# Value and query products of a tile taken in turns into two PSUM banks, in a two-layer attention kernel

## What is computed

```python
xn = layernorm(x) * norm_scale + norm_bias
q, k, v = xn @ Wq + bq, xn @ Wk + bk, xn @ Wv + bv
k, v = masked(k, -inf or -1e6), masked(v, 0)
q = softmax(q per head, over its features)
k = softmax(k per head, over the tokens)
attn = einsum('bhse,bhsd->bhed', k, v)
y = einsum('bhtd,bhed->bhte', q, attn)
scale, shift = split(silu(cond) @ film_emb_W + film_emb_b, 2)
h = layernorm(y) * film_norm_scale + film_norm_bias, then h * (1 + scale) + shift
x = x + silu(h) @ film_out_W + film_out_b
```

## Time and profile before

| | |
|---|---|
| time, median of 3 runs (lowest, highest) | 977.77 us (977.76, 980.23) |
| profiled execution, span from its first to its last instruction | 978.8 us; no time of its own is given beside the span |
| PE busy, weight loads busy | 949.3 us (97%), 819.8 us (84%) |
| DVE, ACT, POOL busy | 828.2 us (85%), 400.9 us (41%), 338.6 us (35%) |
| granted clock, mean over the span | 0.994 |
| chain that ended last, by engine | PE 90%, DVE 4%, issue 2%, others 1% or less |

### The profile page before, as it was taken

How to read it: one execution, slowest core, us unless ns; L and a number is a source line. 1 busy time by engine, 2 the same in 40 slices (tenths; PEclk the granted TensorE clock), 3 DMA queues, 4 the chain that set the end, 5 groups by cost and what they waited for, 6 DMA issues and landing times.

```text
span 978.8 us, 19392 instructions
## 1 busy us (share of the span) xinstructions
PE 949.3 (97%) x7053; PEld 819.8 (84%) x7053; DVE 828.2 (85%) x1690; ACT 400.9 (41%) x809; POOL 338.6 (35%) x441
## 2 busy tenths in 40 slices
PE   4999999999999999999989999999999999999996
PEld 3778888888888888888878888888888888888885
DVE  6799888888988888888998888888888888888865
ACT  4244343343343344334544343343344344344333
POOL 3443233333333333233534433333333333233310
PEclk9899999999999999999999999999999999999999
DMA  8760102010100000000320000000000000000001
GB/s 301 271 221 7 44 7 49 7 50 6 45 7 7 7 7 6 2 6 7 99 75 1 19 26 28 28 17 28 23 17 28 28 18 28 22 18 28 22 13 43
DMA packets 25268, 40.75 MB, mean 42 GB/s; under 512 B 1727, under 2 KB 10039, under 8 KB 25175
## 3 DMA queue, kind: packets, MB, share of 16 engines
q1 hardware_dynamic: 24672, 39.07, 12.0%
q10 hardware_dynamic: 502, 0.46, 0.2%
HBM read 31.13 MB, written 8.39 MB: 40 GB/s over the span
## 4 chain that ended last, share of the span: by engine, by line
PE 90%; DVE 4%; issue 2%; ACT 1%; DMA 1%; POOL 1%; SPq 0%; DVEq 0%; ACTq 0%; POOLq 0%
PE PS L534 69%; PE PS L614 6%; PE PS L636 3%; PE PS L603 3%; PE PS L590 3%; PE PS L575 3%; PE PS L582 3%; DMA STAGE<-in_wk 1%; PE PS L650 1%; DVE XN L754 0%; DVE WL_q L227 0%; PE PS L659 0%; DVE YN L860 0%; ACT WH_k L416 0%; DVE YN L848 0%
## 5 line engine op out<-in xcount | busy, mean ns | idle before, releaser
L421 ACT ACTIVATE EK<-PS 128x512 f32<-128x512 f32 x64 | 38.3, 598 | 391.7 <-PE PS L575 391.7
L534 PE MATMUL PS<-XH,WH_k 128*128 128x256 f32 x512 | 146.8, 287 | 4.2 <-DVE XL L764 4.2
L534 PE MATMUL PS<-XL,WH_k 128*128 128x256 f32 x512 | 146.6, 286 | 0.0
L534 PE MATMUL PS<-XH,WL_k 128*128 128x256 f32 x512 | 146.6, 286 | 0.0
L336 POOL TENSOR_SCALAR VEY<-MVY 128x1 f32<-128x1 f32 x64 | 14.6, 229 | 291.6 <-DVE MVY L855 291.5
L336 POOL TENSOR_SCALAR VEX<-MVX 128x1 f32<-128x1 f32 x64 | 17.5, 273 | 271.4 <-DVE MVX L744 271.2
L534 PE MATMUL PS<-WH_q,XH 128*128 128x512 f32 x256 | 106.4, 416 | 3.6 <-DVE WL_q L227 3.6
L534 PE MATMUL PS<-WH_o,HH 128*128 128x512 f32 x256 | 106.4, 416 | 2.4 <-ACT HH L460 2.4
L534 PEld LDWEIGHTS PS<-XH,WH_k 128*128 128x128 f32 x512 | 99.9, 195 | 7.2 <-ACT XH L479 4.6
L534 PE MATMUL PS<-WH_v,XH 128*128 128x512 f32 x256 | 105.3, 411 | 0.0
L534 PEld LDWEIGHTS PS<-XL,WH_k 128*128 128x128 f32 x512 | 99.8, 195 | 2.3
(11 more groups left out here) (117 smaller groups left out, 2224.7 us busy)
## 6 DMA issues: line engine op xcount, KB each, us to landing
out_x<-X SPq DMA_DIRECT2D x32, 256.0 KB, 2.0
X<-in_film SPq DMA_DIRECT2D x2, 2048.0 KB, 16.9
X<-in_x SPq DMA_DIRECT2D x2, 2048.0 KB, 12.0
STAGE<-in_film SPq DMA_DIRECT2D x4, 1024.0 KB, 6.4
MB<-in_mask SPq DMA_DIRECT2D x30, 128.0 KB, 2.9
X<-in_x SPq DMA_DIRECT2D x3, 1024.0 KB, 15.2
BB<-in_bias_rows SPq DMA_DIRECT2D x6, 256.0 KB, 8.2
STAGE<-in_wk SPq DMA_DIRECT2D x1, 1024.0 KB, 10.3
```

The source lines that it names most:

```text
L421: eng.activation(EK[:, :], PS[:, B_XK, :], ACT.Exp).then_inc(act_ek, 1)
L534: mm = eng.matmul(dst, left[a](c), right[b](c), start=(c == 0 and a + b == 0), stop=(c == C - 1 and a == 1))
```

## The change

B_VO becomes B_V, the values' alone. The output product goes to B_TY, the bank of turned y (for the last three tiles to B_V, B_K and B_Q), so turned y waits for add_x of the tile before, and the output for ACT to have read turned y. In every slot but 0 and 32, values and queries are one loop that issues V and Q in turns, both from the same left operand. It stands where Q stood. On PE, turned keys and queries go ahead of K. On DVE heads moves up to follow keys, x_low goes ahead of h_low, values moves down to stand before queries, and mixed moves behind both, behind late pieces of WL too. On ACT x_turned goes ahead of h_high, and values goes to the end. The core of the diff:

```diff
-            return {t1: B_K, t2: B_Q}.get(o, B_VO)
+            return {t0: B_V, t1: B_K, t2: B_Q}.get(o, B_TY)
...
             def values(i):
                 eng.wait_ge(dve_v, i)
-                if i >= 4:
-                    eng.wait_ge(dve_x, i - 3)
-                project_x(i, 1, bank(B_VO), pe_v)
+                project_x(i, 1, bank(B_V), pe_v)
...
+            def values_and_queries(i):
+
+                g, t = i // 2, i % 2
+                eng.wait_ge(dve_v, i)
+                eng.wait_ge(dve_q, i)
+                eng.wait_ge(act_cp, sum(s <= i for s in FILM_SLOTS))
+                xs = [XH[g % 2], XL[g % 2]]
+                for c in range(C):
+                    for a, b in ((0, 0), (0, 1), (1, 0)):
+                        left = xs[a][:, c, t * T:t * T + T]
+                        first, last = c == 0 and a + b == 0, c == C - 1 and a == 1
+                        mv = eng.matmul(bank(B_V), left, (WH, WL)[b][1][:, c, :], start=first, stop=last)
+                        mq = eng.matmul(bank(B_Q), left, (WH, WL)[b][2][:, c, :], start=first, stop=last)
+                mv.then_inc(pe_v, 1)
+                mq.then_inc(pe_q, 1)
...
             def turn_y(o):
                 eng.wait_ge(dve_yn, o + 1)
                 eng.wait_ge(act_z, o)
+                if o >= 1:
+                    eng.wait_ge(dve_x, min(o, t0))
...
             def output(o):
-                eng.wait_ge(dve_v, min(o + 4, NT))
-                if o == NT - 3:
-                    eng.wait_ge(dve_x, o)
+                if bank_out(o) == B_TY:
+                    eng.wait_ge(act_z, o + 1)
+                    eng.wait_ge(dve_film, sum(s <= o + 3 for s in FILM_SLOTS))
+                else:
+                    eng.wait_ge(dve_v, NT)
+                    eng.wait_ge(dve_q, NT)
```

More of the change, by code:

```diff
@@ L500, in _ @@
                     split_high(w)
-                if 0 < i < NT:
-                    values(i)
+                if m < NSTEP and s > 0:
+                    x_turned(m)
                 if 0 <= o < NT:
                     h_high(o)
-                if m < NSTEP:
+                if s == 0:
                     x_turned(m)
-                if s == 0:
-                    values(0)
+                values(i)
                 for w in SPLIT_LATE.get(s, []) + SPLIT_END.get(s, []):
@@ L670, in _ @@
                 i, j, o, m = s, s - 2, s - 3, s + 2
-                if 0 <= i < NT:
-                    keys(i)
-                if s in FILM_SLOTS:
-                    conditioning(FILM_SLOTS.index(s))
                 if 0 <= j < NT:
@@ L677, in _ @@
                     turn_queries(j)
+                keys(i)
+                if s in FILM_SLOTS:
+                    conditioning(FILM_SLOTS.index(s))
                 if 0 <= o < NT:
                     turn_y(o)
-                if 0 <= i < NT:
-                    values(i)
                 if 0 <= j < NT:
                     attention(j)
+                if i % B == 0:
+                    values(i)
                 if 1 <= s and m < NSTEP:
@@ L693, in _ @@
                     conditioning_fold(FILM_SLOTS.index(s))
-                if 0 <= i < NT:
+                if i % B == 0:
                     queries(i)
+                else:
+                    values_and_queries(i)
                 if s == 0:
@@ L973, in _ @@
                     start_count()
+                if 0 <= j < NT:
+                    heads(j)
                 for n in stats_at(s):
@@ L979, in _ @@
                     split_low(eng, w, LOW_ON_DVE[w])
-                if 1 <= i < NT:
-                    values(i)
-                if 0 <= j < NT:
-                    heads(j)
+                if 0 < s and m < NSTEP:
+                    x_low(m)
                 if 0 <= o < NT:
                     h_low(o)
-                if 0 < s and m < NSTEP:
-                    x_low(m)
                 if s in FILM_SLOTS:
                     conditioning(FILM_SLOTS.index(s))
-                if 0 <= j < NT:
-                    mixed(j)
-                if 0 <= i < NT:
-                    queries(i)
+                if i >= 1:
+                    values(i)
+                queries(i)
                 for w in SPLIT_LATE.get(s, []):
@@ L997, in _ @@
                     x_low(m)
+                if 0 <= j < NT:
+                    mixed(j)
                 if 0 <= o < NT:
```

4 lines of the change are left out of this document (2 added, 2 removed).

## The result

| | before | after |
|---|---|---|
| median (lowest, highest), us | 978.58 of 4 (977.76, 980.23) | 992.26 of 4 (990.84, 997.17) |
| ratio, 95% interval | | 1.0142 [1.0113, 1.017] |
| span of the profiled execution | 978.8 us | 988.5 us (its time 990.84) |
| PE, DVE, POOL busy | 949.3, 828.2, 338.6 us | 947.1, 854.8, 364.3 us |

The account below looks back on a forecast made before the run. PE's issue intervals, without gaps, were taken to bound the kernel. Terms -1 + 6.8 + 1 + 3.8 = +10.6 us on the 978.8 span give 989.4, less 1.0 for the median: 988.4 us, own range 983 to 996, chance 0.62.

Parts of the forecast that it names:

- Intervals: PE's issue intervals: 0 for the alternation; the new order -1 us, between -2 and +1.
- Rival B: Alternating products: changing bank every product shortens the interval, by up to 20.4 us in all; chance 0.14.
- Ordinary slots: The 56 slots without special work: -0.02 us each from the new order, and no new wait.
- rival A: Layer 0, ordinary slots: POOL's bias step delays HL, the output product waits, +17 to +22 us more; chance 0.13.
- Conditioning slots: Slots 6, 9, 12, 15: attention and the fold wait for ACT, 1.7 us a slot, +6.8 in all.
- Slots 1 to 3: First slots: waits for CP and EK, and turned y waiting on mixed; +1 us, between 0 and 3.
- Change of layer: Slots 31 and 32: later turned y, WL pieces and HL; +3.8 us, bounds 1.5 and 6.
- turned y +1.9: Slot 32: mixed, 1.9 us, now stands between WL_v and norm_y, so turned y comes that much later.
- give-back: Slot 32: Q some 3.7 us later, but heads no longer holds up mix by 1.35; leaves +1.8.
- about half a us: Slot 31: the output product waits that much more for HL.
- rival D: Clock: 24 products a slot at 1.2 GHz, each slot 5.1 us longer; chance 0.01.
- Rival C: Conditioning slots' waits half of the forecast, layer change costs nothing: +3 us or less; chance 0.10.

Follow-up runs that it names:

- e1: Changed kernel with the alternation alone undone, twelve value products and then twelve query products: 998.57 us, ratio 1.0189.
- e7: e6 with values and queries as two blocks of twelve instead of alternating: 985.00 us, ratio 1.0062.
- e8: Changed kernel with DVE's statistics of a later x done twice in slots 4 to 28: 1029.11 us, ratio 1.0519.
- e3: Changed kernel with ACT doing both exponents ahead of the copy of the conditioning sums in the six conditioning slots: 991.49 us, ratio 1.0128.
- e5: e3 on the changed kernel, and PE folds the conditioning sums behind values and queries: 989.38 us, ratio 1.0109.
- e9: Kernel before, with PE's values behind attention, turned x and the fold in slots 6, 9, 12, 15: 983.02 us, ratio 1.0041.
- e12: Kernel before, with add_x and norm_y ahead of WL_v's late pieces in slot 31, one WL_q piece on POOL: 977.42 us, ratio 0.999.
- e10: Kernel before, with DVE's mixed behind the late pieces of WL_v in slot 31: 982.53 us, ratio 1.0034.
- e2: Changed kernel with PE's values back ahead of attention in the six conditioning slots, DVE and ACT in the new order: 997.45 us, ratio 1.018.
- e6: Changed kernel with the edits of e5 and e4, and heads behind the middle pieces of WL in slots 31 and 32: 985.07 us, ratio 1.0059.
- e4: Changed kernel with mixed, add_x and norm_y ahead of DVE's late pieces of WL_v in slot 31: 990.91 us, ratio 1.0112.
- e11: Changed kernel with the repairs of e6, fold late only from slot 6, mixed ahead of queries' bias in slot 2: 980.34 us, ratio 1.0011.

## Why the prediction held, and where not

The forecast was 988.4 us and slower, own range 983 to 996; measured 992.26. Point by point:

- **Intervals.** 0.23 us within values and queries: right; e1 and e7 show 0 for the alternation alone. Rival B is out. (Its largest gain was put at 20.4 us; 0.014 x 24 x 62 is 20.8, which changes nothing.) The 0.014 us per product above 512 columns at 2.4 GHz remains, and does not hang on the bank.
- **Ordinary slots.** -0.02 in each of 56, -1 in all: measured -0.03 and -0.02, -1.2.
- **Thin cover (rival A).** HL was to be first by 0.4 us, and was, to the hundredth; the output product waits in no ordinary slot. But e8 shows how near it was: 0.7 us more on DVE cost 1.6 a slot. In one slot rival A did come true: in slot 31 the pieces of WL_k pushed HL behind POOL's bias step (483.34 and 483.95), and HL took 1.75.
- **Conditioning slots.** Forecast +1.7 each, +6.8: measured +1.6 and +6.4. Attention was put at T + 1.1 and T + 2.95 for the fold: 1.06 and 3.03. e3 takes away the first wait, e5 both, e9 brings the second into the kernel before.
- **Slots 1 to 3.** Forecast +1. In the table slots 0 to 3 show +0.2, of which 0.8 is only the place where slots are cut, so -0.6. But the profiled execution of before had lost clock in slot 1: its 24 key products took 5.42 us, in e12 (same order there) 3.05. From the first key product to slot 4, e12 took 56.8 us, the profile of before 58.8. Against e12 the changed kernel is +2.2, less 0.8: +1.4.
- **Change of layer.** Forecast +3.8, bounds 1.5 and 6: measured +5.9. This is the term that was mis-sized. The step that failed was "turned y +1.9". Its wait in slot 32 grew from 1.19 to 5.53 us, by 4.3, where the sum had 3.4: 1.9 for mixed and 1.5 for later pieces of the WL's. Mixed takes 1.84, and the last piece of WL_v starts 4.7 us after the last output product (488.40, 493.11) where it was 3.4 (482.12 and 485.50), so 1.3 later; both were near the sum. The other 1.2 had no place in the sum: DVE now waits for POOL's root ahead of norm_y (0.5), and norm_y is held by POOL's query step (0.6), as e10 shows alone. From turned y to mix it is 10.75 us instead of 10.55, which is heads (WL_q begins 6.3 us after turned y instead of 4.5, 1.8 as forecast) less some 1.6 given back. The 1.9 of the sum's give-back was itself more than its row: mix had waited 1.35, and for the rest the prediction names nothing. Slot 31 gave +1.4 where "about half a us" stood, since HL was held.
- **Not in the sum: the clock.** I had priced it as 24 products a slot in every slot, rival D, and that did not happen: 1.00 through all ordinary slots. What does happen is a loss behind waits: 1.6 us in a conditioning slot of some executions. The changed kernel's four runs had clocks of 0.997, 0.997, 0.990 and 0.993, at 990.8, 991.2, 997.2 and 993.3 us. No trace of the latter two was taken; that they lost the clock in conditioning slots, as e1 and e8 did, is argued, not shown; the start, which also differs from execution to execution, could have done it too.
- **Rival C.** It had the conditioning slots at half of the forecast and the change of layer at nothing. Neither holds: +6.4 and +5.9.

At a clock of 0.997 the kernel takes 991, 2.6 above the forecast and close to what the layer's change was short by, 2.1.

That the two profiled executions differ by 9.7 us, so close to the forecast of 10.6, is partly luck. The profile of before, with its span of 978.8, was one that lost clock at the start (later an execution with that span took 980.7 us); executions of before at a clock of 1.00 had spans of 975.8 to 976.6. Against 976.0 the profiled execution of the changed kernel is 12.5 us longer, so the sum was 1.9 short, about what the change of layer was short by. The forecast time does not carry that piece of luck: it was set against the median of 977.77, a time without the loss, and is 2.4 to 2.8 below the two runs at a clock of 0.997.

## What to carry to other kernels

When one engine issues without a gap and every other one fits beneath it, as here, bringing products together bought nothing; the order could only move covers. So list for each short product what its operand waits for and what large product now stands before it. An order is a property of all the engines: moved on one alone (e2), it made a new and longer wait. And measure the margin rather than the wait: here a chain that ended 0.1 us in time, next to an engine that could block it, was one step of 0.7 us away from 1.6 us a slot.

## What was unexpected of the hardware

- **Some steps of DVE and POOL exclude each other, and the loser's time shows as its own.** Steps with two operands in SBUF took 1.75 (HL) and 1.76 (XL) instead of 0.69 beside POOL's bias step, and norm_y, with one large operand, 1.30 instead of 0.67 beside its query step. POOL's VEX took 0.72 instead of 0.22 beside h_mul. Not every step of DVE does it: in e8 VEX took 0.22 (148.18) while DVE's second statistics ran (148.12 to 148.81). The Trainium skill ("SBUF — State Buffer", "SBUF: two separate sides") calls the shared port pair an exclusive lock, where the loser waits for the whole instruction; the traces agree: VEX ends at 221.76, just behind h_mul at 221.68, and HL of slot 31 at 485.70, 0.5 us behind the bias step at 485.16. Which of the two starts first decides, and 0.4 us decided it here.
- **A wait can cost as much again in clock.** Behind some waits of PE its products ran at the 1.2 GHz level, behind others they did not. The table has all waits above 2.3 us between slots 1 and 62, and a choice of shorter ones:

| wait of PE, us | where | slow products behind it |
|---|---|---|
| 5.23 to 6.12 | slot 32 of the changed kernel (5.53: 5 products) and of e1, e2, e3, e5, e8 | 3 to 10 |
| 4.09 | e10, slot 32 | 9 |
| 3.66 | e5, e6, e7, slot 3 | 6 to 8 |
| 3.00 | e2, slot 3 | 5 |
| 2.64 | e3, slot 3 | none |
| 1.65, and later 2.33 | e4, slot 32 | 8, and 7 |
| 2.13 | e12, slot 32 | 7 |
| 2.09 | e6, e7, e11, slot 32 | none |
| 1.58 to 2.29 | e2, slots 6, 9, 12, 15 | none |
| 1.71 | changed kernel, slot 31 | none |
| 1.25 to 1.48 | e8, 21 slots | none |
| 0.40 and 0.93 | e1, slots 9, 12, 15; e8, slots 9, 12 | 7 or 8 |
| 0.40 and 0.93 | changed kernel and e4, four slots; e1, slot 6; e8, slots 6, 15 | none |
| 0.82 | e9, slots 6, 9, 12, 15 | none |

  So the length of a wait alone does not tell, and what else does stays open. The loss at the start is of this kind: in seven of the fourteen traces, before and e1 among them, a query product of slot 0 had waited 1.56 to 2.07 us for WL_q, and the first 13 to 23 key products of slot 1 were slow; in the other seven that wait was 0.78 to 1.49 and none was. Both orders are in both groups. The Trainium skill ("TensorE: Matmul & The Clock Gate", "HAM oscillation — how this bites in real kernels") describes a loss of clock behind waits on DMA in each pass of a loop; the traces agree in that each wait of 3.66 us or more in the table was followed by one.
- **Where a loss of clock is hidden.** In slot 32 of the changed kernel and in e10 the slow products ran while WL_q was not ready yet, and cost next to nothing: from turned y to mix 10.75 and 10.53 us, where before took 10.55 at full clock. A low clock in the profile is a cost only if nothing else is late.
